# A four-layer graph network on one core: the neighbourhood product moved into the recurrence, and four small jobs moved to other engines

## The chip, the core and the metric

The kernel runs on one core of a Trainium2 chip, as one launch. The metric is the device time of the launch in microseconds (us); lower is better. A core has five engines that run their own instruction streams and meet at semaphores: TensorE (PE in the profile, its weight loads PEld), VectorE (DVE), ScalarE (ACT), GpSimd (POOL) and SyncE (SP), which here only starts transfers. Products are written to PSUM, everything else lies in SBUF, 128 partitions wide.

## The reference, cut to what matters

There are 64 graphs (B) of 128 nodes with 128 features (x: 64x128x128), with a weighted adjacency matrix each (about 6% of the entries are non-zero, the diagonal always). Four layers follow one another, each with a residual and a layer norm:

```
x = layernorm(x + message_passing(x, adj))          # layer 0: per edge exp/softplus filters, products, sum
x = layernorm(x + top8_attention(x, adj))            # layer 1
x = layernorm(x + graph_attention(x, adj, mask))     # layer 2
x = layernorm(x + sigmoid((A_norm @ x) @ lstm(conv(x))))   # layer 3
A_norm = D^-1/2 (A + I) D^-1/2,  D = row sums of A + I
lstm:  128 steps, one after the other, over a batch of 64:
   z = x_t W_ih' + b + h W_hh' ;  i, f, g, o = split(z)
   c = sig(f) c + sig(i) tanh(g) ;  h = sig(o) tanh(c)
```

The change concerns `A_norm @ x`, of which the kernel computes (A + I) @ (x D^-1/2) (called `agg`, 128x128 per graph) ahead of the product with the states of the LSTM; the row sums and their power -1/2 (`deg`, `dinv`); and two things in layer 0: the one-hot matrix by which edges beyond a row's fixed number of slots are added back to their row (`over_t`), and the check that no entry of the adjacency matrix is negative (`least`).

## The kernel before, in words

**Layer 0** (`layer0`, lines 203 to 1024) handles the 64 graphs in a software pipeline. `run` (L345) builds for each engine a body for two graphs; each graph has two units of edges (`k_in` 0 and 1). Some pairs at both ends are written out, the middle runs in a hardware loop (`Fori`, L73), so that addresses there are worked out by register instructions. Per unit ACT computes dist, gauss, expd and hid (L671 to L687), PE the filters `wf` (L782) and the gathered neighbours `rg` (L811), DVE pick, rv and msg (L921, L930, L957), and POOL sums the messages (L569). Per graph DVE also ranks the edges of the graph four ahead (`rank_edges`, L857 to L879), places those that overflow (`place_overflow`, `finish_edges`), and builds `over_t` (L963): a comparison of a row of column numbers with the row number of each overflow edge, 128x132. PE uses it in the product `ub<-over_t,over_u` (L795). ACT reads each adjacency matrix twice (L714, L716): Relu of its negative, and a copy, each with an accumulator that gives the sums of the rows, `least` and `deg`.

Then comes a **check block** (L980 to L1016): DVE gathers whether any graph breaks an assumption (`bad`, `badn`, `flag`; then a dense version of layer 0 would run), and POOL computes `dinv` from `deg` by a power (L1007). Barriers end the block.

**Layers 1 and 2** (`layers12`, L1047 to L1610) go over 16 groups of four graphs, written out in full: each engine's program is a list of operations for `step` 0 to NGR+5, and each operation belongs to the group `step - d` with its own d. The order of the list is the order on the engine. At its end, per group: ACT writes the normalised x3, POOL forms `adj_i` = A' + I (L1177, from transfers of 256 KB started by SP at L1141) and `xs` = x D^-1/2 (L1182), PE forms four products (L1419), ACT copies them to `agg` (L1328). The convolution's products (L1397, L1469) and its copy `dyn` (L1304) are there too.

**The recurrence** (`lstm`, L1614 on) runs 128 steps. Per step PE makes four products of h with 64 columns (L1681: G, I, F, O), then the bias and input products of a later step (L1671, L1673), then two products of zeros, of 512 and 256 columns (L1701, L1702), whose result nobody reads. ACT takes the four tanh and then that of the cell, DVE four operations, the last of which writes h (L1744; the profile calls its buffer `xin`). `quads` (L1656) writes out 16 of the steps and runs 112 in a hardware loop of eight steps a turn.

After it 16 groups of output products, sigmoid, layer norm and the stores.

Of the kernel before, what the change touches and what calls it, by code (L numbers as in the profile page):

```python
# [16 lines left out]
ALU = mybir.AluOpType  # L17
# [61 lines left out]
def build(nc, a, out):  # L79
    offsets, coeff = gaussian_constants()  # L80
    ctx = ExitStack()
    with ctx:
# [25 lines left out]
        bias_parts_in = ctx.enter_context(nc.semaphore("bias_parts_in"))  # L108
        centred = ctx.enter_context(nc.semaphore("centred"))
# [3 lines left out]
        for name, shape in (("wvc", [P, P]), ("w_layer", [P, P + 2]), ("conv_w", [P, 3, P]), ("mask", [P, B]),  # L113
                            ("wqk", [P, P]), ("att_neigh", [P, P]), ("ones", [P, P]),
                            ("gamma4", [P, G, P]), ("beta4", [P, G, P]), ("ident4", [P, G, P])):
            k[name] = sb("m_" + name, shape)
# [86 lines left out]
def layer0(nc, a, k):  # L203
# [49 lines left out]
    least = sb("least", [P, B])  # L253
    over_t = sb("over_t", [P, 2, OPEN_COLS])
# [24 lines left out]
    minus, total = sb("minus", [P, P]), sb("total", [P, P])  # L279
# [23 lines left out]
    def halves(t):  # L303
# [15 lines left out]
        "hits_ready picks_ready edges16 adj_read least_ready "  # L319
# [25 lines left out]
    def run(block, dense):  # L345
# [60 lines left out]
        def _(sp):  # L406
# [51 lines left out]
            def body(pair):  # L458
                for i in range(per_pair):
# [26 lines left out]
                    if i % per_graph == 0:  # L486
                        if not dense and g.static and g.at(4) == 0:
                            sp.dma_start(adj_w[:, 0, :], a["adj_rows"][:, 0, :]).then_inc(adj_in[0], 16)
                        if not dense and g.has(5):
                            after(sp, "adj_read", g, 3, 0)  # L490
                            after(sp, "least_ready", g, 3, 0)
                            alone(sp)
# [21 lines left out]
        def _(pool):  # L514
            if not dense:
# [6 lines left out]
                pool.memset(mln2[:, :], -LN2)  # L522
                pool.memset(k["minus_half"][:, :], -0.5)
# [70 lines left out]
        def _(act):  # L594
            if not dense:
# [47 lines left out]
                act.wait_ge(ident_ready, 1)  # L643
                act.activation(k["ident4"][:, :, :], ident[:, :].unsqueeze(1).broadcast_to((P, G, P)), ACT.Copy)
# [5 lines left out]
            def body(pair):  # L650
                for i in range(per_pair):
# [182 lines left out]
        def _(dve):  # L834
# [62 lines left out]
            def finish_edges(g):  # L897
# [7 lines left out]
                dve.tensor_copy(over_row[:, bass.ds(g.at(4), 1)], p_over[:, 2 * RANKS + 1:2 * RANKS + 2])  # L905
# [6 lines left out]
            def body(pair):  # L912
                for i in range(per_pair):
# [1016 lines left out]
```

## Time and profile before

| | |
|---|---|
| median of 3 runs | 1374.94 us (1372.89 to 1377.21) |
| profiled execution | 1368.68 us, of it span 1366.4 us, TensorE clock 0.957 of full |
| setup | 0 to about 60 us of the span |
| layer 0 | about 60 to 696 us |
| check block and barriers | 696 to 716 us |
| layers 1 and 2 | 716 to 994 us |
| recurrence | 1002.6 to 1314 us |
| output stage | 1314 to 1366 us |
| busy | PE 84%, DVE 68%, ACT 67%, POOL 50% of the span |

The profile is one execution. A row of a timeline gives start, duration, engine, line and operation, and in brackets how long the engine had been idle before it and what it waited for. Consecutive instructions of one engine overlap a little, so the distance of two starts is what an instruction costs its engine, and is less than its duration. Two figures on TensorE's clock occur: full (2.4 GHz) and half (1.2 GHz); the profile gives their mean as the granted clock.

### The profile page before, as it was taken

The page shows a single profiled execution, that of the slowest core. Times are in us where ns is not written, and L with a number is a line of the kernel's source. Part 1 is how long each engine was busy: PE and PEld are TensorE (multiplying, and loading weights), DVE is VectorE, ACT ScalarE, POOL GpSimd, SP SyncE. Part 2 cuts the span into 40 slices and gives each one's busy share as a digit, 9 for nine tenths or more (in the row PEclk, how much of TensorE's full clock was granted, in tenths as well). Part 3 has the DMA queues.
Part 4 walks back from the last instruction along what each step waited for, and adds up shares of the span by engine and source line. Part 5 has one row for each costly group of instructions (what it writes and reads, how often), then busy time and mean ns, then how long its engine had stood idle before and what let it go on. Part 6 is the DMA issues. An engine that isn't in the chain of part 4 may idle for free. (4 is left out here: it accounts for less than half of the span.)

```text
span 1366.4 us, 28761 instructions
## 1 busy us (share of the span) xinstructions
PE 1142.1 (84%) x5996; PEld 752.7 (55%) x6028; DVE 927.6 (68%) x3952; ACT 908.8 (67%) x2636; POOL 686.5 (50%) x1146
## 2 busy tenths in 40 slices
PE   2588889898988888988925789989789999999984
PEld 1244445555544554555514577777666666666673
DVE  3599998988898988889724888788423333333357
ACT  2488888778788878778812778878544444444467
POOL 5266665656665656656755899998500000000026
PEclk9999999999999999999965999999999999999988
DMA  1788677677777886767700111111000000000003
GB/s 47 162 182 193 167 191 168 174 186 163 172 188 167 187 171 173 191 160 177 172 6 21 34 38 39 32 40 32 16 1 0 0 0 0 0 0 0 0 23 102
DMA packets 128163, 129.04 MB, mean 94 GB/s; under 512 B 60867, under 2 KB 107359, under 8 KB 128097
## 3 DMA queue, kind: packets, MB, share of 16 engines
q1 hardware_dynamic: 126372, 127.19, 38.8%
q10 hardware_dynamic: 1725, 1.13, 0.3%
q8 instruction: 23, 0.38, 0.1%
q14 instruction: 43, 0.35, 0.1%
HBM read 123.05 MB, written 5.21 MB: 94 GB/s over the span
## 5 line engine op out<-in xcount | busy, mean ns | idle before, releaser
L782 PE MATMUL wf<-hid,w2t 128*128 128x384 f32 x512 | 209.3, 534 | 61.6 <-DVE msg L957 61.6
L569 POOL TENSOR_TENSOR sum<-msg 128x384 f32<-128x384 f32 (+1 forms) x128 | 146.5, 1145 | 74.4 <-DVE msg L957 73.9
L782 PEld LDWEIGHTS wf<-hid,w2t 128*128 128x128 f32 x512 | 89.9, 195 | 138.3 <-issue 106.5
L1787 POOL MEMSET r_minus_half<- 128x4 f32 x1 | 0.1, 102 | 324.7 <-POOLq L1653 324.7
L957 DVE SCALAR_TENSOR_TENSOR msg<-wf,b2c,rv 128x768 f32<-128x768 f32 x128 | 130.0, 1015 | 14.6 <-PE wf L782 14.2
L1735 DVE SCALAR_TENSOR_TENSOR r_new<-r_gates 128x64 f32<-128x64 f32 x128 | 28.9, 226 | 149.9 <-ACT r_gates L1715 149.9
L682 ACT ACTIVATE expd<-zb,safe_b,reached 128x768 f32<-128x768 f32 x128 | 124.9, 976 | 1.8 <-PE zb L768 1.8
L930 DVE TENSOR_TENSOR rv<-rg,sq_bc 128x768 f32<-128x768 f32 x128 | 121.4, 948 | 1.7 <-PE rg L811 1.4
L1681 PE MATMUL r_zgo<-xin,w_hh 128*128 (+1 forms) x508 | 110.2, 299 | 14.0 <-DVE xin L1744 1.8
L687 ACT ACTIVATE hid<-expd 128x768 f32<-128x768 f32 x128 | 108.0, 844 | 17.7
L767 PE MATMUL zb<-gauss,w1t 64*128 64x384 f32 x256 | 117.5, 540 | 0.0
L768 PE MATMUL zb<-gauss,w1t 64*128 64x384 f32 x256 | 117.5, 540 | 0.0
L1713 ACT ACTIVATE r_gates<-r_zgo 128x64 f32<-128x64 f32 x128 | 28.7, 224 | 123.3 <-PE r_zgo L1681 123.3
L1681 PEld LDWEIGHTS r_zgo<-xin,w_hh 128*128 128x128 f32 x508 | 76.2, 189 | 62.2 <-issue 54.7
L552 POOL TENSOR_TENSOR rf_r<-rf,rf_hi 128x128 f32<-128x128 f32 x64 | 27.5, 429 | 149.5 <-ACT rf_hi L707 149.5
L811 PE MATMUL rg<-pick,rf_hi 128*128 128x384 bf16 x256 | 84.9, 332 | 0.0
L811 PE MATMUL rg<-pick,rf_mid 128*128 128x384 bf16 x256 | 84.2, 329 | 0.0
L811 PE MATMUL rg<-pick,rf_lo 128*128 128x384 bf16 x256 | 83.8, 327 | 0.0
L671 ACT ACTIVATE dist<-val_bc,noff_c 128x384 f32<-128x384 f32 x128 | 77.2, 603 | 0.0
L921 DVE TENSOR_SCALAR pick<-idx_bc,iota_col 128x768 bf16<-128x768 bf16 x128 | 66.2, 517 | 9.6 <-issue 9.6
L675 ACT ACTIVATE gauss<-dist 128x384 f32<-128x384 f32 x128 | 66.9, 523 | 6.2
L1744 DVE SCALAR_TENSOR_TENSOR xin<-r_gates,r_tanh_c 128x64 f32 (+1 forms) x128 | 28.8, 225 | 53.4 <-ACT r_tanh_c L1721 53.4
(300 smaller groups left out, 3297.5 us busy)
## 6 DMA issues: line engine op xcount, KB each, us to landing
sq_bc<-edge_sq SPq DMA_DIRECT2D x64, 768.0 KB, 4.4
val_bc<-edge_val SPq DMA_DIRECT2D x128, 192.0 KB, 4.6
idx_bc<-edge_idx SPq DMA_DIRECT2D x64, 384.0 KB, 5.5
adj_w<-in_adj_rows SPq DMA_DIRECT2D x64, 64.0 KB, 5.2
xt_w<-in_x_cols SPq DMA_DIRECT2D x64, 64.0 KB, 4.8
xin<-in_x_rows SPq DMA_DIRECT2D x32, 128.0 KB, 4.7
m_adj_g<-in_adj_rows SPq DMA_DIRECT2D x16, 256.0 KB, 2.7
m_adjt_g<-in_adj_t SPq DMA_DIRECT2D x16, 256.0 KB, 2.7
```

Of the source, the lines that this page charges most:

```text
L569: pool.tensor_tensor(sum1[:, 0:wide, :], m[:, 0:wide, :], m[:, wide:2 * wide, :], ALU.add)\
L671: act.activation(dist2[:, :], val_bc[:, q, :], ACT.Square, bias=noff_c[:, :])\
L675: act.activation(gauss[:, u.mod(2, 2), :], dist2[:, :], ACT.Exp, scale=coeff)\
L682: act.activation(expd[:, :].rearrange("p (a n) -> p a n", a=2), zb[:, :, 0:HALF], ACT.Exp, bias=safe_b1[:, :], scale=reached[:, :]).then_i ...
L687: act.activation(hid[:, u.mod(2, 1), :], expd[:, :], ACT.Ln, bias=1.0)\
L767: pe.matmul(zb[:, 0, 0:HALF], w1t[0:NG, :], gauss[0:NG, qn, :], start=True, stop=True)
L768: pe.matmul(zb[:, 1, 0:HALF], w1t[NG:P, :], gauss[NG:P, qn, :], start=True, stop=True)\
L782: last = pe.matmul(wf[:, half, 0:HALF], w2t[:, :], hid[:, q, half * HALF:(half + 1) * HALF], start=True, stop=True)
L811: last = pe.matmul(rg[:, half, 0:HALF], part[:, gn.mod(2), :], picked, start=part is rf_hi, stop=part is rf_lo)
L930: dve.tensor_tensor(halves(rv[:, u.mod(2), :]), rg[:, :, 0:HALF], halves(sq_bc[:, u.mod(UNIT_BUFS), :]), ALU.mult).then_inc(s["rv_ready"], 1)
L957: dve.scalar_tensor_tensor(halves(msg[:, q, :]), wf[:, :, 0:HALF], b2c[:, :], halves(rv[:, q, :]), ALU.add, ALU.mult)\
L1681: pe.matmul(z_of(bank, q)[:, j, :], w_hh[:, q, :], h, start=False, stop=True, skip_group_check=True).then_inc(ready, 1)
```

## The change

Seven edits:

1. **Neighbourhood product.** `adj_i`, its transfers, the four products per group and their copy leave `layers12`; POOL's product of x and D^-1/2 now writes to `agg` directly. In the recurrence each step has one f32 product of 128 columns: on even steps A' by this `agg`, on odd steps the identity by it, added in the same PSUM tile (A x + x). After the odd step's tanh ACT copies the tile over `agg` of that graph. The two zero products become one of 256 columns.
2. **Transfers.** SP starts 128 KB (two graphs of A') every four steps, after the product that has read the half buffer; the first two come at the end of `layers12`.
3. **Recurrence written out.** `quads` is a plain Python loop: all 128 steps are in the program.
4. **One-hot.** `over_t` is no longer a comparison on DVE but two operations of ACT: |column - row|, then Relu(1 - that). DVE writes the row number with a minus sign instead of copying it.
5. **Sign check.** ACT's Relu with accumulator goes; POOL compares the matrix with zero and adds the result to a running sum (two operations of 128x128 per graph). DVE reduces that sum in the check block.
6. **Degree power.** POOL's power becomes exp(-0.5 ln d) in two operations of ACT; POOL multiplies as before.
7. **Order in layers 1 and 2.** The lists of POOL, ACT, PE and DVE are in another order, with other distances d, over NGR+7 steps instead of NGR+6.

```diff
@@ layer 0, POOL, ACT, DVE
+                    if not dense and k_in == 1 and g.has(4):
+                        q = g.mod(2, 4)
+                        pool.wait_ge(adj_in[q], g.pair * 16 + 16 * ((g.inner + 4) // 2 + 1))
+                        if not g.static or g.at(4) >= 1:
+                            w(pool, "negative_ready", g.at(4))
+                        pool.sem_inc(k["held"]["Pool"], 1)
+                        pool.tensor_scalar(below_zero[:, :], adj_w[:, q, :], 0.0, None, ALU.is_lt)\
+                            .then_inc(s["below_ready"], 1)
+                        w(pool, "below_ready", g.at(4) + 1)
+                        pool.tensor_tensor(negatives[:, :], negatives[:, :], below_zero[:, :], ALU.add)\
+                            .then_inc(s["negative_ready"], 1)
...
-                act.activation(k["ident4"][:, :, :], ident[:, :].unsqueeze(1).broadcast_to((P, G, P)), ACT.Copy)
...
-                        act.activation(minus[:, :], adj_w[:, q, :], ACT.Relu, scale=-1.0,
-                                       accum_out=least[:, bass.ds(g.at(4), 1)])
...
+                    if not dense and k_in == 0 and g.has(0):
+                        w(act, "row_ready", g.at() + 1)
+                        after(act, "over_t_ready", g, -1, 0)
+                        act.activation(over_gap[:, :], iota_row[:, :], ACT.Abs, bias=over_row[:, bass.ds(g.at(), 1)])\
+                            .then_inc(s["gap_ready"], 1)
+                        w(act, "gap_ready", g.at() + 1)
+                        after(act, "u_ready", g, -2, 0)
+                        act.activation(over_t[:, g.mod(2), :], over_gap[:, :], ACT.Relu, scale=-1.0, bias=1.0)\
+                            .then_inc(s["over_t_ready"], 1)
...
-                    if not dense and k_in == 1 and g.has(0):
-
-                        after(dve, "u_ready", g, -2, 0)
-                        dve.tensor_scalar(over_t[:, g.mod(2), :], iota_parts[:, :, 0:OPEN_COLS // 3],
-                                          over_row[:, bass.ds(g.at(), 1)], None, ALU.is_equal)\
-                            .then_inc(s["over_t_ready"], 1)
@@ check block
-            pool.tensor_tensor(dpow[:, :], dsafe[:, :], k["minus_half"][:, :], ALU.pow).then_inc(powers[2], 1)
...
+            act.activation(dlog[:, :], dsafe[:, :], ACT.Ln).then_inc(log_ready, 1)
+            act.wait_ge(log_ready, 1)
+            act.activation(dpow[:, :], dlog[:, :], ACT.Exp, scale=-0.5).then_inc(pow_ready, 1)
@@ layers12, POOL
-                        pool.tensor_tensor(adj_i[:, :, :], adjt_g[:, g % 2, :, :], ident4[:, :, :], ALU.add).then_inc(s["adj_i"], 1)
...
-                        pool.tensor_tensor(xs[:, :, :], xres[:, g * G:(g + 1) * G, 1:P + 1],
+                        pool.tensor_tensor(agg[:, g * G:(g + 1) * G, :], xres[:, g * G:(g + 1) * G, 1:P + 1],
@@ recurrence
             def quads(eng, body):
 
-                body(0, 0, True, False)
-                body(4, 1, False, False)
-                with eng.Fori(1, P // 8 - 1) as pair:
-                    body(pair * 8, 0, False, False)
-                    body(pair * 8 + 4, 1, False, False)
-                body(P - 8, 0, False, False)
-                body(P - 4, 1, False, True)
+                for pair in range(P // 8):
+                    body(pair, 0, pair == 0, False)
+                    body(pair, 1, False, pair == P // 8 - 1)
+
+            @block.sync
+            def _(sp):
+                def body(pair, bank, first, final):
+                    if pair < P // 8 - 1:
+                        sp.wait_ge(agg_p, pair * 4 + (bank * 2 + 2))
+                        sp.sem_inc(held["SP"], 1)
+                        sp.dma_start(adjt[:, bank, :, :], a["adj_t"][:, pair * 4 + 4 + bank * 2:pair * 4 + 6 + bank * 2, :])\
+                            .then_inc(adjt_in[bank], 16)
+                quads(sp, body)
...
-                        pe.matmul(idle_p[:, :], idle[:, 0:P], idle[:, :], start=True, stop=True)
-                        pe.matmul(idle_p[:, 0:2 * P], idle[:, 0:P], idle[:, 0:2 * P], start=True, stop=True)
+                        graph = pair * 4 + (bank * 2 + j // 2)
+                        if j == 0:
+                            pe.wait_ge(adjt_in[bank], pair * 16 + 16)
+                        if j % 2 == 0:
+                            if not (first and j == 0):
+                                pe.wait_ge(agg_ready, graph)
+                            pe.matmul(p_agg[:, 0, :], agg[:, graph, :],
+                                      adjt[:, bank, j // 2, :], start=True, stop=False)
+                        else:
+                            pe.matmul(p_agg[:, 0, :], agg[:, graph, :],
+                                      ident[:, :], start=False, stop=True).then_inc(agg_p, 1)
+                        pe.matmul(idle_p[:, 0:256], idle[:, 0:P], idle[:, 0:256], start=True, stop=True)
...
+                        if j % 2 == 1:
+                            graph = pair * 4 + (bank * 2 + j // 2)
+                            act.wait_ge(agg_p, graph + 1)
+                            act.activation(agg[:, graph, :], p_agg[:, 0, :],
+                                           ACT.Copy).then_inc(agg_ready, 1)
```

The order on the engines shows three places. On DVE in layer 0, inside the hardware loop, around the second message of a graph (msg L957 before, L979 after), the rows were:

```order
L894 SCALAR_TENSOR_TENSOR slot_of<-iota_row,over_end,mb 128x128
L957 SCALAR_TENSOR_TENSOR msg<-wf,b2c,rv 128x768
L963 ISA
L963 TENSOR_SCALAR over_t<-iota_parts,over_row 128x132
L903 SCALAR_TENSOR_TENSOR rank_hit<-mb,iota_col,minus_rank 128x13
L905 REGISTER_ALU
L905 COPY over_row<-mb 128x1
```

and are now, with the same neighbours:

```order
L915 SCALAR_TENSOR_TENSOR slot_of<-iota_row,over_end,mb 128x128
L979 SCALAR_TENSOR_TENSOR msg<-wf,b2c,rv 128x768
L924 SCALAR_TENSOR_TENSOR rank_hit<-mb,iota_col,minus_rank 128x13
L926 REGISTER_ALU
L926 TENSOR_SCALAR over_row<-mb 128x1
```

The one-hot is gone from between the message and rank_hit, and the copy of the row number is a multiplication of the same 128x1. The second place is POOL in the middle of layers 1 and 2, from the shift of the second norm on. Before:

```order
L1160 TENSOR_SCALAR m_shift_n<-m_mv_n 128x4
L1165 TENSOR_TENSOR m_rstd_n<-m_veps_n,minus_half 128x4
L1171 TENSOR_TENSOR m_offset_n<-m_shift_n,m_rstd_n 128x4
L1177 TENSOR_TENSOR m_adj_i<-m_adjt_g,m_ident 128x512
L1182 TENSOR_TENSOR m_xs<-xres,dinv 128x512
L1190 TENSOR_TENSOR m_veps_no<-m_mv_no,m_eps_sum 128x4
L1195 TENSOR_TENSOR m_rstd_no<-m_veps_no,minus_half 128x4
L1200 TENSOR_TENSOR m_x1b<-xin,m_beta 128x512
```

and after:

```order
L1200 TENSOR_TENSOR m_rstd_n<-m_veps_n,minus_half 128x4
L1204 TENSOR_SCALAR m_shift_n<-m_mv_n 128x4
L1210 TENSOR_TENSOR m_offset_n<-m_shift_n,m_rstd_n 128x4
L1215 TENSOR_TENSOR m_x1b<-xin,m_beta 128x512
L1220 TENSOR_TENSOR agg<-xres,dinv 128x512
L1228 TENSOR_TENSOR m_veps_no<-m_mv_no,m_eps_sum 128x4
L1233 TENSOR_TENSOR m_rstd_no<-m_veps_no,minus_half 128x4
```

One operation of 128x512 has gone, and x1b stands ahead of the product with dinv. The third place is PE in the recurrence, one step inside the hardware loop (ISA and REGISTER_ALU rows work out addresses). Before:

```order
L1681 ISA
L1681 MATMUL r_zgo<-xin,w_hh 128x64
L1681 MATMUL r_zi<-xin,w_hh 128x64
L1681 MATMUL r_zf<-xin,w_hh 128x64
L1680 REGISTER_ALU
L1681 MATMUL r_zgo<-xin,w_hh 128x64
L1671 MATMUL r_zgo<-gate_ones,bias_parts 128x256
L1673 ISA
L1673 MATMUL r_zgo<-dyn,w_ih 128x256
L1701 MATMUL r_idle_p<-r_idle 128x512
L1702 MATMUL r_idle_p<-r_idle 128x256
```

and after, one odd step:

```order
L1686 MATMUL r_zgo<-xin,w_hh 128x64
L1686 MATMUL r_zi<-xin,w_hh 128x64
L1686 MATMUL r_zf<-xin,w_hh 128x64
L1686 MATMUL r_zgo<-xin,w_hh 128x64
L1676 MATMUL r_zgo<-gate_ones,bias_parts 128x256
L1678 MATMUL r_zgo<-dyn,w_ih 128x256
L1716 MATMUL r_o<-ident,agg 128x128
L1718 MATMUL r_idle_p<-r_idle 128x256
```

No address work is left, and the f32 product (its PSUM tile is called r_o) stands where the zero product of 512 columns stood.

## Rows read from the trace of the kernel before

**Rows 1.** Stages by windows: stretch, length, busy of each engine, clock, DMA share.

```profile
60.00:640.00 580.00, 510.61 (x2352) 291.81 (x2350) 520.16 (x2007) 464.53 (x1148) 357.02 (x634) 0.97 0.75 178
790.00:939.00 149.00, 137.10 (x950) 108.51 (x949) 121.33 (x626) 120.16 (x361) 141.69 (x211) 1.00 0.12 37
...
1020.00:1300.00 280.00, 266.26 (x1461) 185.87 (x1489) 94.72 (x457) 131.49 (x571) 0.00 (x0) 1.00 0.00 0
1304.00:1314.00 10.00, 7.92 (x41) 5.74 (x40) 3.42 (x17) 4.61 (x20) 0.00 (x0) 0.75 0.00 0
```

**Rows 2.** Waits in layer 0, 400.2 to 451.25: total us, times, longest.

```profile
DVE over_bits L874 <- DVE found L871: 1.2, 5, 0.2
...
PE wf L782 <- DVE msg L957: 5.8, 5, 1.3
...
ACT squares L663 <- DVE over_pick L908: 4.2, 5, 0.9
...
POOL rf_r L552 <- ACT rf_hi L707: 9.4, 5, 1.9
```

**Rows 3.** Layer 0, DVE: line L963 (396 to 440, then whole), and its timeline.

```profile
L963 DVE TENSOR_SCALAR over_t<-iota_parts,over_row x5: 341/342/342, 396.6 to 436.3; 128x132 f32<-128x132 f32 x5
...
L963 DVEq FUSED_REGOPS  x56: 46/46/46, 82.8 to 638.5; - x56
...
406.81 0.34 DVE L963 TENSOR_SCALAR over_t<-iota_parts,over_row 128x132 f32<-128x132 f32 x1
407.07 0.22 DVE L903 SCALAR_TENSOR_TENSOR rank_hit<-mb,iota_col,minus_rank 128x13 f32<-128x13 f32 x1
...
407.52 0.56 DVE L921 TENSOR_SCALAR pick<-idx_bc,iota_col 128x768 bf16<-128x768 bf16 x1
...
413.26 0.41 DVE L921 TENSOR_SCALAR pick<-idx_bc,iota_col 128x768 bf16<-128x768 bf16 x1
```

**Rows 4.** Layer 0, timelines of ACT and POOL: operations of 128x128.

```profile
406.28 0.31 ACT L724 ACTIVATE t_ex<-t_ab 128x128 f32<-128x128 f32 x1
...
408.47 0.52 POOL L581 TENSOR_TENSOR sum<-sum,msg 128x128 f32<-128x128 f32 x1
```

**Rows 5.** Check block, timeline.

```profile
696.75 10.59 POOL L1007 TENSOR_TENSOR dpow<-dsafe,minus_half 128x64 f32<-128x64 f32 x1
...
697.10 0.15 DVE L1000 CAST flag<-mb 1x1 int32<-1x1 f32 x1 [0.28 <-PE mb L1016]
```

**Rows 6.** Layers 1 and 2: POOL's timeline, a wait in 780 to 926, and the last group's products.

```profile
878.98 1.27 POOL L1177 TENSOR_TENSOR m_adj_i<-m_adjt_g,m_ident 128x512 f32<-128x512 f32 x1
880.20 1.04 POOL L1182 TENSOR_TENSOR m_xs<-xres,dinv 128x512 f32<-128x512 f32 x1
...
893.89 1.27 POOL L1177 TENSOR_TENSOR m_adj_i<-m_adjt_g,m_ident 128x512 f32<-128x512 f32 x1
...
PE m_p_t L1380 <- POOL xin L1246: 11.2, 10, 1.3
...
992.27 1.06 PE L1419 MATMUL m_p_two<-m_adj_i,m_xs 128*128 128x128 f32 x8
```

**Rows 7.** Recurrence: line L1744 in the loop and written out; timeline of one step.

```profile
L1744 DVE SCALAR_TENSOR_TENSOR xin<-r_gates,r_tanh_c x9: 224/225/226, 1020.3 to 1039.9; 128x64 f32 x8, 128x64 f32<-128x64 f32 x1
L1744 DVEq FUSED_REGOPS  x8: 57/57/71, 1022.7 to 1039.8; - x8
...
L1744 DVE SCALAR_TENSOR_TENSOR xin<-r_gates,r_tanh_c x4: 224/225/226, 1004.5 to 1011.3; 128x64 f32<-128x64 f32 x4
...
1301.40 0.38 PE L1701 MATMUL r_idle_p<-r_idle 128*128 128x512 bf16 x1
1301.62 0.27 PE L1702 MATMUL r_idle_p<-r_idle 128*128 128x256 bf16 x1
1301.80 0.30 PEld L1681 LDWEIGHTS r_zgo<-xin,w_hh 128*128 128x128 f32 x2 [0.30 <-DVE xin L1744]
1302.28 0.22 ACT L1713 ACTIVATE r_gates<-r_zgo 128x64 f32<-128x64 f32 x1 [0.79 <-PE r_zgo L1681]
```

More of the change, by code:

```diff
@@ L1471, in _ @@
                         last.then_inc(s["conv_a"], 1)
+                    g = step - 3
+                    if 0 <= g < NGR:
+                        for j in range(G):
+                            last = pe.matmul(p_val[:, j, :], x1t[:, j, :], wvc[:, :], start=True, stop=True)
+                        last.then_inc(s["val_p"], 1)
+                    g = step - 3
+                    if 0 <= g < NGR:
+                        w(pe, "prob", g)
+                        w(pe, "e2t", g - 3)
+                        for j in range(G):
+                            last = pe.transpose(p_pt[:, j, :], prob[:, j, :], ident[:, :])
+                        last.then_inc(s["probt_p"], 1)
@@ new lines, in _ @@
+                    g = step - 6
+                    if 0 <= g < NGR:
+                        w(pe, "hl", g + 1)
+                        w(pe, "e2t", g)
+                        for j in range(G):
+                            last = pe.matmul(p_o2[:, j, :], e2t[:, j, :], hl[:, g % HL_BUFS, j, :], start=True, stop=True)
+                        last.then_inc(s["o2_p"], 1)
+                    g = step - 2
+                    if 0 <= g < NGR:
+                        w(pe, "x1", g)
+                        w(pe, "probt", g - 1)
+                        for j in range(G):
+                            last = pe.transpose(p_x1t[:, j, :], x1[:, j, :], ident[:, :])
+                        last.then_inc(s["x1t_p"], 1)
@@ new lines, in _ @@
+                    g = step - 3
+                    if 0 <= g < NGR:
+                        w(pe, "probt", g)
+                        w(pe, "val", g)
+                        for j in range(G):
+                            last = pe.matmul(p_o1[:, j, :], prob_t[:, j, :], val[:, j, :], start=True, stop=True)
+                        last.then_inc(s["o1_p"], 1)
+                    g = step - 2
+                    if 0 <= g < NGR:
+                        w(pe, "x1t", g)
+                        pe.matmul(p_qt[:, :, :], wqk[:, :], x1t[:, :, :], start=True, stop=True).then_inc(s["qt_p"], 1)
@@ new lines, in _ @@
+                    g = step - 7
+                    if 0 <= g < NGR:
+                        w(pe, "conv_a", g)
+                        for j in range(G // 2, G):
+                            for kk in range(3):
+                                last = pe.matmul(p_conv[:, j, :], xres[:, g * G + j, kk:kk + P], conv_w[:, kk, :], start=False,
+                                                 stop=kk == 2, skip_group_check=True)
+                        last.then_inc(s["conv_p"], 1)
+                    g = step - 4
@@ new lines, in _ @@
+                    if 0 <= g < NGR:
+                        w(pe, "x2", g)
+                        for j in range(G):
+                            last = pe.transpose(p_x2t[:, j, :], x2[:, g % X2_BUFS, j, :], ident[:, :])
+                        last.then_inc(s["x2t_p"], 1)
+                    g = step - 2
+                    if 0 <= g < NGR:
+                        w(pe, "qt", g)
+                        for j in range(G):
+                            last = pe.matmul(p_s[:, j, :], qt[:, j, :], x1t[:, j, :], start=True, stop=True)
+                        last.then_inc(s["s_p"], 1)
@@ L1706, in _, with body @@
             def _(act):
-                def body(t, bank, first, final):
+                def body(pair, bank, first, final):
+                    t = pair * 8 + bank * 4
                     for j in range(4):
```

512 lines of the change are left out of this document (223 added, 289 removed).

## The prediction

> **What bounds the kernel now.** I read the windows by stage first, then the waits of each engine inside a stage, then the timeline of the engine that does not wait. The chain of waits on the page is of no help here: the stages meet at barriers, so each stage has its own bound and the whole is their sum.
>
> Layer 0: from 60 to 640 PE, DVE and ACT are all busy for over 80% of the stretch, so busy time alone decides nothing [rows 1]. The waits do: in five graphs PE waits for DVE's message 5.8 us, ACT for DVE's over_pick 4.2, POOL for ACT's rf_hi 9.4, while the longest wait of DVE is for an earlier result of its own, 1.2 in all [rows 2]. DVE sets the pace. Its line L963 starts five times between 396.6 and 436.3, thus 9.92 us a graph; over the whole loop (82.8 to 638.5, 56 starts) it is 10.10 [rows 3]. The difference, 55 x 0.18 = 10 us, I put down to TensorE's clock, which is 0.97 over the stage [rows 1], so that some 35 of the 580 us ran at half clock.
>
> Check block: POOL's power takes 10.59 us alone, from 696.75, and the flag is known at 697.25; everything behind waits for POOL [rows 5].
>
> Layers 1 and 2: from 790 to 939 POOL is busy 141.69 of 149 us, more than PE (137.10), DVE and ACT [rows 1]; a turn (L1177 to L1177) takes 14.91, and PE waits for POOL's x1 11.2 us in ten groups [rows 6]. POOL sets the pace.
>
> Recurrence: nothing is saturated in the sense of throughput; it is a ring PE, ACT, DVE, ACT, DVE, PE. In the hardware loop a step takes (1039.9 - 1020.3)/8 = 2.45 us, in the written-out part (1011.3 - 1004.5)/3 = 2.27, with the same operations; only the loop has the register operations beside them [rows 7].
>
> **The change part by part.** All durations are of the profiled execution, whose own time is 1368.7 us; the median of the runs is 1374.94, 6.3 above it.
>
> *One-hot off DVE.* The row 406.81 is followed by the next at 407.07, so the operation costs DVE 0.26 [rows 3]. What it feeds had waited for DVE in turn; what could be late instead is PE's result for rank_hit (DVE issues it 0.26 earlier) and rg for rv, and before either had DVE waiting in these rows nothing is seen of a wait. 56 graphs in the loop and two before it: 58 x 0.26 = 15 us. I count none for the last six graphs, which rank no edges. If DVE meets a new wait at once: 0; if the register operation in front of it also counts, 58 x 0.30 = 17. ACT gets two operations of 128x128 of about 0.31 to 0.34 start to start [rows 4] and loses one with its accumulator (I take the same 0.3): net +0.4 a graph, against 0.84 a graph that it waits for over_pick alone [rows 2]; hidden. Without that cover 58 x 0.4 = +23. The product that uses over_t comes some 3 us after ACT makes it, so no wait of PE is added. I take -15.
>
> *Sign check on POOL.* Two operations of about 0.5 (as the sum of two 128x128 tiles, 0.52 [rows 4]) and a wait for itself of some 0.15: 1.2 us a graph. They stand in k_in 1 ahead of the message's sum, and POOL waits for rf_hi 1.9 us a graph [rows 2]; hidden in length. What is queued behind: the sum of a message, which frees the msg buffer two units on. 0 taken, bounds 0 and 58 x 0.3 = +17. SP's load of the next adjacency matrix waits for POOL too, but is four graphs ahead.
>
> *A rule against this.* DVE's pick takes 0.56 us in one unit and 0.41 in the other, for the same 128x768 [rows 3]; something beside it stretches it, and POOL, which would be busy 1.0 us more of each 9.9, may be that. If that second message, pick or another operation is lengthened as pick is, by 0.15 once a graph, the price is 58 x 0.15 = +9 us. The Trainium skill ("SBUF — State Buffer", section "SBUF: two separate sides") says that VectorE in its two-port modes, or with two SBUF inputs, and GpSimd take one port pair in turn, as a lock held for the whole instruction, and the loser blocks. The trace agrees in direction only: 0.15 us is less than a whole operation of POOL (0.52 [rows 4]) would block. By that rule at its hardest a blocked DVE operation would wait up to 0.5 us a graph, and the 15 us would turn into +14.
>
> *Clock in layer 0.* The 10 us are lost at half clock. Work will be denser by 2.6%, which speaks for fewer falls, but no row shows when one comes. Bounds -10 and +5; I take -5.
>
> *Degree power.* The dinv chain becomes dsafe, Ln, Exp, multiply, each under 0.5 us, and would end about 697.3; the flag comes 0.4 later than 697.25 because of one more reduce and wait, thus 697.65. Before, the power ended at 697.34 + 10 and the multiply at about 707.8. Gain 10.1 [rows 5]; bounds 8.5 (a table of ACT to be loaded) and 10.5.
>
> *Layers 1 and 2.* POOL loses L1177, 880.20 - 878.98 = 1.22 a turn; x D^-1/2 stays (1.04) [rows 6]. A turn would be 14.91 - 1.22 = 13.7. PE would then need 137.10/149 x 14.91 = 13.7 less the four products, 1.06 at most: 12.7 [rows 1, 6]. So POOL still sets the pace, narrowly. Ten steady turns give 12, all sixteen 20; at the end the products and their copy go too, but the convolution's copy stays last, and one more step of distance was put in. I take -15. The other end: the order of all four engines is new, and an order in which one wait of 1.2 us a turn comes back gives 0; below -20 I see no reason.
>
> *Recurrence, written out.* 112 steps x (2.45 - 2.27) = 20.5; over the whole loop I get the same with 2.26, 21. I take -21; if register work is not the cause, 0.
>
> *Recurrence, product.* The zero product of 512 columns costs 0.22 (1301.40 to 1301.62), the 256-column one about half of it, so PE is free near 1301.73 and starts on h at 1301.80 [rows 7]. A f32 product of 128x128 costs at most 1.06/4 = 0.27 and, without the last one's tail, 0.24 [rows 6]: +0.02 to +0.05, against 0.07 of room. Bounds 0 and +0.05 x 128 = 6; I take +3. ACT's copy on odd steps (0.31 at most [rows 4]) can start when the product is done, about 1301.8, and ends by 1302.15; ACT's next tanh is at 1302.28 and ACT had been idle 0.79 before it [rows 7]: nothing, and if it were late by 0.1 on 64 steps, +6. PE's wait for that copy is a whole step away. The transfers, 128 KB each four steps (9 us) with no other traffic, are nothing. Queued behind a late one would be PE's whole ring.
>
> Sum: -15 - 5 - 10 - 15 - 21 + 3 = -63. From 1368.7 that is 1305.7 for the profiled execution, and from the median 1374.9 it is 1312.
>
> **The rivals.**
> (a) *Layer 0 gives nothing*: ACT or POOL becomes the bound, or the shared use with POOL eats it. For: three engines above 80% [rows 1], pick's 0.56. Against: the waits of 0.84 and 1.9 us a graph. Then 15 of -63 go, and the clock's 5 too: 1332.
> (b) *Layers 1 and 2 keep their pace*: the new order puts a wait where adj_i was. For: PE is only 0.3 us a group behind POOL in busy time, and everything is moved. Then 1327.
> (c) *The loop was not the cause*: a written-out step stays at 2.45, for instance because the slow steps come with the middle of the run and not with the registers. Against: 56 to 57 ns of register operations in front of L1744 [rows 7]. Then 1333.
> (d) *The f32 product is late for h* by 0.1 a step: +13 instead of +3, 1322.
> (e) *Slower than before*: TensorE falls to half clock within the recurrence. From 1020 to 1300 the clock is 1.00 with PE busy 266 of 280 us; from 1304 to 1314, where input products are missing, it is 0.75 [rows 1]. The zero product of 512 columns, which keeps PE busy, is replaced by a f32 one of 128. A step at half clock costs between nothing and 2.26 us more; I take 1.4. From 63/1.4 = 45 of 128 steps at half clock the kernel is slower; with half the steps at half clock it is 1312 + 90 = 1402. Against it: the new product keeps the array as long as the old (0.24 for 0.22), and a step is shorter, so PE is denser.
>
> **How the numbers follow.** Forecast 0.60 (1312; its own range 1303 to 1321), (a) 0.14, (b) 0.10, (c) 0.06, (d) 0.04, (e) 0.06. A difference of 0.3% (4 us) is what a measurement of this kernel can tell. (a) to (d) all stay faster, also two of them together (1347). Of (e) a third is short enough to leave it faster or the same. Faster 0.95, same 0.01, slower 0.04. The range: low end with layer 0's clock falls gone (-5), layers 1 and 2 at their full 20 (-5) and no cost of the product (-3), 1299; high end with (a), (b) or (c) alone, 1333.
>
> **What would show it.** Layer 0: DVE at about 9.66 a graph in a stretch at full clock, rank_hit 0.26 earlier after msg; wrong if DVE shows waits for PE or ACT over 0.3 us a graph. Check block: layers 1 and 2 start about 10 us after the multiply's former distance, near 8 us behind the flag. Layers 1 and 2: period 13.7 on POOL, with POOL still without waits; wrong if POOL waits. Recurrence: 2.26 to 2.30 a step throughout, clock 1.00, ACT idle about 0.4 instead of 0.79 before the tanh of even steps; wrong if PE's wait for h is gone (then PE is late itself). The forecast as a whole is wrong if the recurrence shows clocks under 1.00 or if two stages give back nothing.

## The result and the profile after

The changed kernel takes 1324.41 us (median of 4 runs, 1322.82 to 1328.99) against 1376.08 before; ratio 0.963 with a 95% interval of 0.960 to 0.966. That is 52 us less. Forecast was 1312 with a range of 1299 to 1333: right in direction and within the range, 12 us too hopeful, and 3 us above the 1303 to 1321 that the prediction gave its own forecast. Measured again beside the experiments, it took 1320.39 against 1370.14 (0.963, 0.960 to 0.966).

The program's stages are separated by barriers, so the two profiled executions can be set side by side. Layer 0 is counted to the start of `dsafe`, the check block to the first instruction of layers 1 and 2, these to the first state of the recurrence, the recurrence to its last state, output to the end of the span (us):

| kernel | layer 0 | check | layers 1, 2 | recurrence | output | span |
|---|---|---|---|---|---|---|
| before | 695.8 | 19.9 | 288.8 | 309.3 | 52.6 | 1366.4 |
| changed | 693.7 | 9.9 | 279.0 | 288.9 | 55.7 | 1327.2 |
| difference | -2.1 | -10.0 | -9.8 | -20.4 | +3.1 | -39.2 |
| forecast | -20 | -10 | -15 | -18 | 0 | -63 |

The profiled execution was the slowest of its four, by 4 to 6 us. Check block and recurrence stand almost as forecast, layers 1 and 2 lack a third, and layer 0 lacks nearly all. Output, which the change leaves alone, lost 3.

The check block, timeline of the changed kernel (start, duration, engine, line; idle before in brackets):

```profile
693.73 0.47 POOL L1024 TENSOR_SCALAR dsafe<-deg 128x64 f32<-128x64 f32 x1 [3.86 <-SPq L996]
...
694.24 0.26 ACT L1034 ACTIVATE dlog<-dsafe 128x64 f32<-128x64 f32 x1 [2.40 <-POOL dsafe L1024]
...
694.52 0.26 ACT L1036 ACTIVATE dpow<-dlog 128x64 f32<-128x64 f32 x1
...
694.97 0.32 POOL L1029 TENSOR_TENSOR dinv<-dpow,dpos 128x64 f32<-128x64 f32 x1 [0.21 <-ACT dpow L1036]
...
695.40 0.15 DVE L1020 CAST flag<-mb 1x1 int32<-1x1 f32 x1 [0.28 <-PE mb L1041]
```

Where 10.59 us of POOL stood [rows 5], two operations of 0.26 us stand, and the flag is last, as forecast. The recurrence, one odd step of the changed kernel:

```profile
1098.18 0.38 PE L1716 MATMUL r_o<-ident,agg 128*128 128x128 f32 x2
...
1098.30 0.22 DVE L1767 SCALAR_TENSOR_TENSOR xin<-r_gates,r_tanh_c 128x64 f32<-128x64 f32 x1 [0.32 <-ACT r_tanh_c L1738]
1098.40 0.27 PE L1718 MATMUL r_idle_p<-r_idle 128*128 128x256 bf16 x1
1098.58 0.30 PEld L1686 LDWEIGHTS r_zgo<-xin,w_hh 128*128 128x128 f32 x2 [0.19 <-DVE xin L1767]
...
1098.60 0.28 ACT L1742 ACTIVATE agg<-r_o 128x128 f32<-128x128 f32 x1 [0.33 <-PE r_o L1716]
...
1099.05 0.23 ACT L1730 ACTIVATE r_gates<-r_zgo 128x64 f32<-128x64 f32 x1 [0.17 <-PE r_zgo L1686]
```

It answers to [rows 7]: the f32 product costs PE 0.22 (1098.18 to 1098.40), exactly what the zero product of 512 columns cost; DVE's operation that writes h starts at 1098.30 and PE starts on h at 1098.58, the same 0.28 as before (1301.52 and 1301.80). ACT's copy lies in a gap of which 0.17 us is left. Steps follow at 2.26 us in the median; four of them take 2.49 to 2.92, the last two of these at the very end, as before. TensorE's granted clock is 1.00 from 1000 to 1262 us.

Layers 1 and 2: POOL in two successive turns of the changed kernel.

```profile
845.64 1.04 POOL L1220 TENSOR_TENSOR agg<-xres,dinv 128x512 f32<-128x512 f32 x1
...
859.25 1.04 POOL L1220 TENSOR_TENSOR agg<-xres,dinv 128x512 f32<-128x512 f32 x1
```

A turn takes 13.61 where it took 14.91 [rows 6]: 1.3 us less, against 1.2 in the forecast. Sixteen products with dinv span 185.5 us (777.7 to 963.2) instead of 198.2. Behind the last one 17.9 us pass to the recurrence's first tanh, instead of 14.1. The step of distance that was put in is not the reason: the experiment three_edits below, which has layers 1 and 2 as before, needs 17.2. What differs is TensorE's granted clock (the figure before the last two), in that stretch of the kernel before and of three_edits:

```profile
988.90:1003.00 14.10, 10.85 (x56) 6.96 (x56) 0.46 (x3) 2.81 (x4) 1.01 (x1) 1.00 0.00 1
```
```profile
954.60:971.70 17.10, 13.86 (x55) 9.06 (x56) 0.46 (x3) 2.92 (x3) 0.99 (x1) 0.80 0.01 1
```

The twelve products of the convolution in it take PE 1.60 us before and 2.93 in three_edits. In the changed kernel the clock there is 0.73, and 0.71 to 0.80 in all the others. Why the profiled execution of the kernel before kept the full clock here is open.

Layer 0, stretch and waits of DVE (the same columns as in [rows 1, 2]):

```profile
60.00:640.00 580.00, 503.84 (x2375) 287.96 (x2376) 510.92 (x1968) 479.94 (x1160) 417.58 (x755) 0.99 0.89 179
```
```profile
DVE over_bits L895 <- DVE found L892: 14.5, 59, 0.3
DVE found L878 <- DMA adj_w<-in_adj_rows: 12.6, 12, 2.4
DVE msg L979 <- PE wf L803: 10.0, 10, 1.3
```

The clock has risen from 0.97 to 0.99, as hoped, and the one-hot is gone from DVE; but 12.6 us of waits for the adjacency matrix are new (0.5 before), and POOL is busy 418 us instead of 357. The experiments look for the rest.

### The profile page after: what moved, and what is told of

Its sections match the earlier page's. It is cut to its first block and busy times, and to the rows that moved or that the text cites. A ratio compares the mean times of both kernels' runs of the same rounds, so it can differ in the third digit from the quotient of the medians.

```text
span 1327.2 us, 28584 instructions
## 1 busy us (share of the span) xinstructions
PE 1120.4 (84%) x6028; PEld 770.1 (58%) x6028; DVE 918.7 (69%) x3889; ACT 929.1 (70%) x2685; POOL 723.0 (54%) x1258
## 5 line engine op out<-in xcount | busy, mean ns | idle before, releaser
L803 PE MATMUL wf<-hid,w2t 128*128 128x384 f32 x512 | 201.0, 516 | 61.2 <-DVE msg L979 61.2
L585 POOL TENSOR_TENSOR sum<-msg 128x384 f32<-128x384 f32 (+1 forms) x128 | 150.4, 1175 | 29.0 <-DVE msg L979 28.4
L979 DVE SCALAR_TENSOR_TENSOR msg<-wf,b2c,rv 128x768 f32<-128x768 f32 x128 | 129.8, 1014 | 10.0 <-PE wf L803 10.0
L1686 PE MATMUL r_zgo<-xin,w_hh 128*128 128x64 f32 x508 | 111.2, 301 | 2.0 <-DVE xin L1767 1.8
L588 POOL TENSOR_TENSOR sum<-sum 128x128 f32<-128x128 f32 x128 | 58.6, 458 | 10.0
```

The costliest lines, as they stand in the source:

```text
L585: pool.tensor_tensor(sum1[:, 0:wide, :], m[:, 0:wide, :], m[:, wide:2 * wide, :], ALU.add)\
L803: last = pe.matmul(wf[:, half, 0:HALF], w2t[:, :], hid[:, q, half * HALF:(half + 1) * HALF], start=True, stop=True)
L979: dve.scalar_tensor_tensor(halves(msg[:, q, :]), wf[:, :, 0:HALF], b2c[:, :], halves(rv[:, q, :]), ALU.add, ALU.mult)\
L1686: pe.matmul(z_of(bank, q)[:, j, :], w_hh[:, q, :], h, start=False, stop=True, skip_group_check=True).then_inc(ready, 1)
```

## The experiments

All times are medians beside runs of the kernel before on the same chip (1369 to 1370 us); stages and rows are from one profiled execution each. The diffs are shortened. **First group**: the changed kernel again, three of its edits alone, and its sign check at two other places.

**after_again**, no edit.

> The changed kernel, unchanged, once more, for a second profile of it. Its first profile lost 12.6 us in 12 waits of DVE (found) for the transfer of adj_w, with landing times of 6.5 us instead of 5.2, a DMA share of 0.90 instead of 0.75 in 60 to 640, and 0.24 us a group in the output stage. Theory 1 (the kernel does it: its transfers or their order collide): the waits for adj_w are there again, 8 us or more in all, and the output stage again takes about 55.7 us from the last state of the recurrence. Theory 2 (that execution was slow by itself, as its 1329 us against 1323 to 1325 of the other three suggests): the waits for adj_w fall under 4 us and the time of the profiled execution is about 1323.

1320.39 us, span of the profile 1319.4, waits for adj_w 0.7 us. So the 12.6 us belong to that execution and not to the kernel as such (theory 2); why the transfers were late then stays open. But layer 0 still took 688.3 us, 13 more than -20 would leave, with no wait to show for it; and output again took 55.6 (theory 1). What had grown in this execution is one duration. DVE's pick (126 in layer 0):

```profile
L943 DVE TENSOR_SCALAR pick<-idx_bc,iota_col 128x768 bf16<-128x768 bf16 x126 | 79.7, 632 | 9.6 <-PE rg L832 9.6
```

632 ns in the mean; in the kernel before 518. In the timeline:

```profile
382.13 0.45 POOL L555 TENSOR_TENSOR negatives<-negatives,below_zero 128x128 f32<-128x128 f32 x1
...
382.50 1.14 DVE L943 TENSOR_SCALAR pick<-idx_bc,iota_col 128x768 bf16<-128x768 bf16 x1
382.55 0.88 POOL L585 TENSOR_TENSOR sum<-msg 128x256 f32<-128x256 f32 x1
```

Pick ends at 383.64, 0.21 after POOL's sum ends (383.43), and takes 1.14 us instead of 0.41. The sum starts only at 382.55, because the two operations of the sign check stand in front of it on POOL. DVE does not "wait" in any view; the operation is just longer.

The sum's row starts 0.05 us behind pick's, and at that distance either can lose. The first profile of the changed kernel has pairs like this one:

```profile
385.11 0.42 DVE L943 TENSOR_SCALAR pick<-idx_bc,iota_col 128x768 bf16<-128x768 bf16 x1
```
```profile
385.17 1.12 POOL L585 TENSOR_TENSOR sum<-msg 128x256 f32<-128x256 f32 x1
```

Here pick takes its 0.42 and the sum is longer, 1.12 for 0.88. Over both profiles, where the sum starts 0.020 to 0.050 us behind pick, pick takes 1.12 to 1.15 (35 pairs); where it starts 0.049 to 0.066 behind, the sum takes 1.10 to 1.12 and pick 0.42 (21 pairs). In after_again pick loses 27 of 29 such pairs, in the first profile 8 of 27, so that its mean is 537 ns there. Layer 0 of the first profile is thus long for other reasons in the main: against sign_early below it has 22 us more, of them 12 of waits for adj_w, 4 of waits for PE and 3 of pick.

**three_edits**, the kernel before with one edit each in layer 0, check block and recurrence (the sign check stays on ACT, both zero products stay):

```diff
-  over_t = iota == over_row                 (DVE)
+  over_gap = Abs(iota - row); over_t = Relu(1 - over_gap)   (ACT)
-  dpow = pow(dsafe, -0.5)                   (POOL)
+  dpow = Exp(-0.5 * Ln(dsafe))              (ACT)
-  with eng.Fori(1, P // 8 - 1) as pair: ...
+  for pair in range(P // 8): ...
```

> The kernel before with three of the edits, which lie in three different stages: over_t built on ACT (layer 0), the degree power on ACT (check block), and the recurrence written out, with both zero products and no f32 product. Everything else as before. If the terms of the prediction add up stage by stage: layer 0 is 12 to 15 us shorter, check block 10, recurrence 21, in all -45, about 1330. If the waits for adj_w come from ACT, whose read of adj_w stands behind the two new operations, they appear here too (6 us or more), and layer 0 gives only 4 to 8; if they come from the sign check on POOL they do not appear.

1316.47 us, ratio 0.960 (0.956 to 0.963): as fast as the whole change, or a little faster, without the new product and without the new order. Layer 0 672.6 (-23), check 9.5 (-10), recurrence 288.4 (-21). A graph takes DVE 9.68 us over the loop, where the forecast had 9.66 at full clock, and the granted clock is 1.00 in 60 to 640. So the one-hot gives its 15 us and the falls of the clock besides, and something else in the change takes 16 us of it back. Layer 0 gives more than the 12 to 15 of the expectation, and the whole 54 us instead of 45. Waits for adj_w: 1.2 us. Output takes 55.7 us here too, so that its 3 us come neither from the new product nor from the new order.

**sign_early**: the changed kernel, POOL's sign check moved.

```diff
-                    if not dense and k_in == 1 and g.has(4):      # POOL, sign check
+                    if not dense and k_in == 0 and g.has(4):
```

> The changed kernel with POOL's two operations of the sign check moved from k_in 1 to the head of k_in 0, where POOL waits for rf_hi 1.5 us a graph. The semaphore that SP needs for the next adjacency matrix then comes some 5 us earlier. If that semaphore delays the load: the waits of DVE for adj_w vanish and the time falls by about 10 us, to 1313. If the load is late because transfers themselves take longer (landing 6.5 instead of 5.2 us), nothing changes within 3 us.

1304.20 us, 0.953 (0.949 to 0.957): 16 us less than the changed kernel, layer 0 671.7. The gain came, but not for the reason that I had written beside it: the load was not late in after_again either. It is pick:

```profile
424.79 0.53 POOL L552 TENSOR_SCALAR below_zero<-adj_w 128x128 f32<-128x128 f32 x1
425.40 0.46 POOL L555 TENSOR_TENSOR negatives<-negatives,below_zero 128x128 f32<-128x128 f32 x1
...
431.53 0.87 POOL L585 TENSOR_TENSOR sum<-msg 128x256 f32<-128x256 f32 x1 [0.67 <-DVE msg L979]
...
431.81 0.81 DVE L943 TENSOR_SCALAR pick<-idx_bc,iota_col 128x768 bf16<-128x768 bf16 x1
```
```profile
L943 DVE TENSOR_SCALAR pick<-idx_bc,iota_col 128x768 bf16<-128x768 bf16 x126 | 64.9, 515 | 9.6 <-PE rg L832 9.6
```

The same two operations of POOL now lie in its wait for rf_hi; the sum starts earlier, pick ends 0.22 after it again, but is held for less time: 515 ns in the mean. 126 x (0.632 - 0.515) = 14.7 us, against 16.6 us between the two layers 0 (688.3 and 671.7). Over the loop the two agree closely: a graph takes 9.93 us in after_again and 9.68 here, and its two picks together 1.27 and 1.03, while DVE's idle time is 0.58 in both.

**sign_act**: the check back on ACT, nothing on POOL.

```diff
+  act.activation(minus, adj_w[q], ACT.Relu, scale=-1.0, accum_out=least[g])   # ACT
-  pool.tensor_scalar(below_zero, adj_w[q], 0.0, None, ALU.is_lt)              # POOL
-  pool.tensor_tensor(negatives, negatives, below_zero, ALU.add)
```

> The changed kernel with the sign check back on ACT (Relu with accumulator, as before) and no operation of it on POOL. If POOL's two operations are what stretches the transfers or the other engines: DMA share and landing times fall back to those of before (0.75, 5.2 us), the waits for adj_w vanish, 1313. If ACT is so full that the sign check there costs its 0.3 us a graph: about +10, 1334. If it is neither: 1324 within 3.

1304.68 us (0.952, 0.948 to 0.955), below all three cases of the expectation; layer 0 672.5, pick 516 ns. Moving the sign check to POOL was thus worth nothing at the better of its two places and cost 16 us at the place the change gave it. The DMA share (0.80) says nothing: it is 0.75 to 0.89 over the kernels with no relation to their times. Against three_edits this kernel differs by the moved product with its transfers and by the new order alone: its median is 11.8 us less, and its layers 1 and 2 are 15.5 us shorter in the profile.

**Second group**, all with sign_early's sign check.

**out_wait**:

```diff
                        before(dve, "y_act", g - 2)
+                        before(dve, "veps_ready", g)
                        dve.tensor_tensor(r3[:, q3, :, :], act_out[:, q, :, :], xres[...], ALU.add)
```

> The kernel with the sign check at the head of POOL's k_in 0 (sign_early, 1304.2), and in the output stage one more wait of DVE: the sum r_r of a group starts only after POOL's veps of the group before. In the changed kernel, and in every variant since, the output stage takes 55.6 us from the last state on, in the kernel before 52.6, with the same code. The traces show POOL's veps taking 0.69 us where it starts just behind the start of DVE's r_r (two SBUF operands, 0.68) and ending with it, and 0.33 where it starts ahead of it. If that order is the cause: veps 0.2 to 0.35, a group takes about 2.5 instead of 2.79 us, the stage 52 to 53. If the cause is elsewhere (addresses, clock), the stage stays at 55.6 or grows with the wait.

A miss: the stage takes 58.0 us and the kernel 1308.12 (0.954, 0.952 to 0.957). But its trace shows the mechanism at another operation. Rows of one group, first of the kernel before, then of the changed one, then of out_wait:

```profile
1347.39 0.33 POOL L1793 TENSOR_SCALAR r_veps<-r_mv 128x4 f32<-128x4 f32 x1
...
1347.60 0.68 DVE L1860 TENSOR_TENSOR r_r<-r_act_out,xres 128x512 f32<-128x512 f32 x1
1347.99 1.18 POOL L1798 TENSOR_TENSOR r_rstd<-r_veps,r_minus_half 128x4 f32<-128x4 f32 x1 [0.27 <-POOL r_veps L1793]
```
```profile
1304.31 0.68 DVE L1883 TENSOR_TENSOR r_r<-r_act_out,xres 128x512 f32<-128x512 f32 x1
1304.38 0.69 POOL L1816 TENSOR_SCALAR r_veps<-r_mv 128x4 f32<-128x4 f32 x1
...
1305.35 1.04 POOL L1821 TENSOR_TENSOR r_rstd<-r_veps,r_minus_half 128x4 f32<-128x4 f32 x1 [0.28 <-ACT r_y L1871]
```
```profile
1295.69 0.69 DVE L1884 TENSOR_TENSOR r_r<-r_act_out,xres 128x512 f32<-128x512 f32 x1 [0.29 <-POOL r_veps L1816]
1295.72 1.56 POOL L1821 TENSOR_TENSOR r_rstd<-r_veps,r_minus_half 128x4 f32<-128x4 f32 x1 [0.28 <-POOL r_veps L1816]
```

An operation of POOL that starts while DVE's r_r runs is the longer, the earlier it starts: rstd by 0.14 (1.18 for 1.04) before, veps by 0.36 (0.69 for 0.33) in the changed kernel, rstd by 0.52 in out_wait. Its end is tied to the end of r_r: rstd ends 0.89 to 0.90 us behind it, whether it started 0.40 or 0.03 behind r_r's start. A group takes 2.55, 2.79 and 2.93 us. The three stages have the same operations; they differ in where POOL meets r_r.

**rv_first**: rv ahead of pick in DVE's k_in 0.

```diff
-                    if u.has(1): ... pick(u + 1)
-                    if u.has(0): ... rv(u)
+                    if u.has(0): ... rv(u)
+                    if u.has(1): ... pick(u + 1)
```

> sign_early with the order of two operations of DVE exchanged in k_in 0 of layer 0: rv ahead of pick. In sign_early pick takes 0.41 us three times in two graphs and 0.81 once, and that one overlaps POOL's sum of 0.87; in the changed kernel 1.14, 0.41, 0.63, 0.41. If pick and POOL's operation exclude one another (pick ends 0.2 us after POOL's operation ends): in the new place, 0.9 later, pick takes 0.41 to 0.5 each time, and layer 0 is up to 58 x 0.2 = 12 us shorter, 1293 to 1300. If DVE meets another wait instead (pick is later for PE's rg), no gain or a loss of some us: 1304 to 1310.

1309.28 us (0.957, 0.955 to 0.959), layer 0 674.1: no gain, as in the second case of the expectation. Pick falls to 445 ns in the mean, but DVE now stands for PE:

```profile
DVE rv L953 <- PE rg L832: 13.4, 31, 0.5
```

**old_order**: sign_early with layers 1 and 2 as before on every engine, less what belongs to adj_i:

```diff
-  g = step - 6: POOL adj_i = adjt + ident4 ; PE p_agg = xs @ adj_i ; ACT agg = p_agg
-  POOL xs = xres * dinv
+  POOL agg = xres * dinv                     (order of all other operations as in the kernel before)
```

> sign_early with the order of layers 1 and 2 as in the kernel before, on every engine, but without adj_i, its transfers, the four products and their copy. If only the removal counts: turns of 13.7 us on POOL and a shorter drain (one step less), the stage within 2 us of sign_early's 273.6. If the new order was needed for the gain: POOL waits in each turn, turns of 14.0 to 14.9, 5 to 15 us more.

1315.80 us (0.961, 0.959 to 0.963). Layers 1 and 2 take 289.2 us, as long as with adj_i (288.8, and 291.1 in three_edits), and 11 more than the other kernels of this group (277.9 to 278.1). The whole kernel takes 6 to 10 us more than they do. A turn takes 14.48, and POOL waits in every turn for something that it had hardly waited for before:

```profile
860.72 1.04 POOL L1194 TENSOR_TENSOR agg<-xres,dinv 128x512 f32<-128x512 f32 x1
862.55 0.20 POOL L1202 TENSOR_TENSOR m_veps_no<-m_mv_no,m_eps_sum 128x4 f32<-128x4 f32 x1 [0.79 <-DVE m_mv_no L1534]
```
```profile
POOL m_veps_no L1202 <- DVE m_mv_no L1534: 7.9, 10, 0.8
```

0.79 of the 1.22 us that POOL saved are spent waiting for DVE's mv_no, which used to be hidden behind adj_i. A turn keeps 0.43 of them, 3.5 us over the sixteen products (194.7 for 198.2), and the end of the stage, at a granted clock of 0.73 instead of 1.00, takes as much back (18.1 us for 14.1). So by these rows the removal alone is worth 4 us at best; with the new order the stage is 11 to 15 us shorter. The new order without the removal was not run.

**no_zero**: no zero product in the recurrence.

```diff
-                        pe.matmul(idle_p[:, 0:256], idle[:, 0:P], idle[:, 0:256], start=True, stop=True)
```

> sign_early without the zero product of 256 columns in the recurrence. If the zero product only fills time, 0 to -1 us. If it keeps TensorE's clock up: the granted clock of 1020 to 1250 falls below 1.00 and steps at half clock take about 0.6 us or more longer, up to +80 us over 128 steps. This prices the rival in which the clock falls in the recurrence.

1306.10 us (0.953, 0.952 to 0.955); recurrence 289.7 us, as in out_wait and old_order of this group (289.0 in sign_early), granted clock:

```profile
1000.00:1240.00 240.00, 237.24 (x1375) 191.30 (x1376) 87.88 (x423) 136.43 (x582) 0.00 (x0) 1.00 0.05 15
```

The clock stays at its full level without it, with PE busy 237 of 240 us. Rival (e) had no ground in this kernel.

**Third group**: sign_early again, and a last test of the output stage.

> sign_early once more, beside the next kernel: the same as before, 1302 to 1308, output stage 55.6 us after the last state, 2.79 a group.

1305.28 us (0.952, 0.949 to 0.954). Its profiled output stage took 53.6 us, not the 55.6 expected, and a group 2.55: here POOL's rstd is the stretched one (1.19 us in the mean). The same program falls into one pattern or another.

**act_psum**: the sigmoid's result in PSUM.

```diff
-        lw, act_out = (sb(n, [P, 2, G, P]) for n in ("lw", "act_out"))
+        lw = sb("lw", [P, 2, G, P])
+        act_out = [z_i[i][...] for i in range(2)]      # two idle PSUM banks, P x G x P each
```

> sign_early with the result of the sigmoid in the output stage in PSUM (two banks that are idle there) instead of SBUF, so that DVE's sum r_r reads one SBUF operand and one PSUM operand instead of two SBUF operands. So far a group takes 2.42 us plus what r_r adds to POOL's operation that starts while it runs: 0.13 before (rstd 1.17 instead of 1.04, group 2.55), 0.36 in the changed kernel (veps 0.69 instead of 0.33, group 2.79), 0.52 in out_wait (rstd 1.56, group 2.93). If r_r with two SBUF operands is what holds POOL off: veps at most 0.33, rstd 1.04, a group 2.42, the stage 50 to 51, in all 4 to 6 us less than sign_early. If the overlap in time alone stretches POOL, or something else sets the 2.79: stage 55 to 56, time as sign_early within 2.

```profile
1283.42 0.33 POOL L1817 TENSOR_SCALAR r_veps<-r_mv 128x4 f32<-128x4 f32 x1 [0.21 <-DVE r_mv L1896]
1283.63 0.68 DVE L1884 TENSOR_TENSOR r_r<-r_zi,xres 128x512 f32<-128x512 f32 x1
1284.02 1.04 POOL L1822 TENSOR_TENSOR r_rstd<-r_veps,r_minus_half 128x4 f32<-128x4 f32 x1 [0.27 <-POOL r_veps L1817]
```

The same overlap as in the kernel before (rstd starts 0.39 after r_r, which takes 0.68), and rstd takes 1.04, not 1.18, as it does in all 16 groups: with one operand in PSUM r_r holds nobody off. A group takes 2.55 us, though, as in the kernel before and in sign_early2, and not the 2.42 expected: POOL now waits for DVE (0.21), whose own operations fill the 2.55. The stage takes 52.5 us, 1 less than in sign_early2 and not the 50 to 51 expected; the 0.14 that rstd loses shortens no group of 2.55, and whether the edit rules out the pattern of 2.79 one execution can't show. In all 1302.95 us (0.951, 0.950 to 0.953), the lowest median measured, though it can't be told from sign_early2 by its time. Both beat the kernel before and the changed kernel (1324.41 and 1320.39).

## Why the prediction was right, and where it was not

The direction, and the terms of the check block, the recurrence and the one-hot, came out by the mechanisms named. That the total fell within the range is in part luck: two costs that stood in the sum with nothing, the sign check's and the output stage's, were covered by a range drawn for a whole stage that gives nothing back, and layer 0's clock and the recurrence gave a few us more than was counted.

- **Check block, -10.** Right: -10.0 in the profile, -10.4 in three_edits.
- **Recurrence written out, -21.** Right: -20.9 as one edit (309.3 to 288.4). Rival (c) falls. That it is the register operations, and not something else of the loop, is argued from [rows 7] and was not tested apart.
- **f32 product, +3.** Too high: 0.22 us as the zero product it replaces, and three_edits to sign_act, 288.4 to 288.6, is +0.2 for 128 steps. Rival (d) falls, and (e) with no_zero.
- **One-hot, -15, and clock, -5.** Right as edits: together -23 in three_edits, with 9.68 us a graph for 9.66 forecast, and a clock of 1.00, which took back most of the 10 us.
- **Sign check, 0.** This is the term that failed; by itself it is more than the 12 us that the forecast lacks. I wrote "hidden in length", from POOL's waits. In length it is hidden; but it shifts POOL's sum against DVE's pick. I had the row (pick 0.56 and 0.41), named the mechanism, priced it at 0.15 us a graph, or 0.5 at its hardest, and then left it out of the sum, since "the trace agrees in direction only". Measured in after_again: 0.25 us a graph. The error was to judge a lock by one row of how long it held: pick takes 0.41 when it comes first and up to 1.15 when it does not. The sign that I had named, waits of DVE, could not show it. The price is 16 us (after_again against sign_early and sign_act). In the first profile pick won most of these meetings, and late transfers and other waits cost that execution about as much; they are not explained.
- **Layers 1 and 2, -15.** The size of a turn was right (13.61 for 13.7). The profile shows -9.8, against -11 to -15 in other executions: the sixteen products give 12.6, and 3.8 us go to a longer end of the stage. I had looked for that in the added step; it is TensorE's clock there, for which I had no term. The reason was only half right: I credited the removal of adj_i, with the new order as a risk (rival b). In old_order the removal alone gives 0.43 of its 1.22 us a turn, and it takes the new order to get the rest.
- **Output, 0.** It lost 3 us in the profile, without any edit to it, by the phase in which POOL meets r_r. I had no term for it.

The page "SBUF — State Buffer" of the Trainium skill (section "SBUF: two separate sides") has the rule that covers both places: one shared port pair, held by whoever comes first for its whole instruction, by VectorE in a two-port mode or, against a GpSimd operation that reads SBUF, with two SBUF inputs. The runs agree with it in who is held up: either pick or the sum, never both, with the change-over where the sum starts 0.05 us behind pick; POOL's operations are stretched by 0.14 to 0.52 us beside a sum of two SBUF operands, and by nothing beside the same sum with one operand in PSUM. They differ in how much: by the rule the loser is blocked altogether until the other ends, and would need its full time from there. Measured, a pick of 0.41 ends 0.21 to 0.22 us behind the sum that held it up, in every kernel, and a rstd of 1.04 ends 0.90 behind r_r. That pick runs in a two-port mode no view shows. In the prediction I had set the rule aside.

What stays open: why the transfers of adj_w were late in one execution of the changed kernel and not in the next; why TensorE's clock is lower at the end of layers 1 and 2 in every kernel but the one before; what the new order alone would give; and why the output stage settles in one pattern or another.

## What to carry to other kernels

An operation added to an idle engine is not free because it fits into the idle time: ask what it moves, and whether the moved operation shares something with the engine that sets the pace. Such sharing shows in no wait, only in the durations of one line: compare minimum and maximum, and read the partner engine's rows at the same time. And when work is taken off the pacing engine, look for the operation that waits next and expect the gain only once the order has been redone.

## What the runs showed of the hardware

DVE's 128x768 bf16 comparison takes 0.41 us alone and up to 1.15 us against a POOL operation of 0.88 us, whose row may start up to 0.05 us later; where it starts 0.05 to 0.07 later, the comparison takes 0.42 and POOL's operation 1.10 to 1.12. Where the comparison is the one held up, it ends 0.21 to 0.22 us behind POOL's operation. A POOL operation of 1.04 us takes up to 1.56 us beside a DVE sum of two f32 SBUF operands of 128x512 (0.68 us) and ends 0.90 behind it; it takes 1.04 where one of the operands is in PSUM. In the recurrence a written-out step takes 2.26 us, one in a hardware loop 2.45. A f32 product of 128x128 takes PE as long, start to start, as a bf16 one of 512 columns (0.22 us).
